# Eleven of 71 expert tiles spread over two step pairs, 16-bit routing marks, and the last values inside the branch arms

## What is computed

```python
x = L0_attn_x                        # (4, 1024, 128) f32
xn = _layernorm(x, axis=-1)
x = x + _L0_attn_ref(xn, W_q, W_k, W_v, W_o) + _L0_ffn_ref(xn, Wg, gamma, beta, W1, b1, W2, b2)
```

## Time and profile before

| | |
|---|---|
| median of 3 runs | 589.49 us (587.09 to 590.52) |
| the profiled execution | 589.15 us, its span 587.2 us |
| PE busy | 92% |
| ACT busy | 85% |
| DVE busy | 51% |
| POOL busy | 42% |
| TensorE clock, mean granted | 0.992 |

### The profile page before, as it was taken

How to read it: one execution, slowest core, us unless ns; L and a number is a source line. 1 busy time by engine, 2 the same in 40 slices (tenths; PEclk the granted TensorE clock), 3 DMA queues, 4 the chain that set the end, 5 groups by cost and what they waited for, 6 DMA issues and landing times.

```text
span 587.2 us, 12446 instructions
## 1 busy us (share of the span) xinstructions
PE 541.0 (92%) x4620; PEld 246.0 (42%) x4620; DVE 300.9 (51%) x1002; ACT 501.4 (85%) x552; POOL 246.0 (42%) x303
## 2 busy tenths in 40 slices
PE   8899988878999999999899999999989999999783
PEld 6323312222455554445345555434534555554111
DVE  4975789965434344463344433555433444343672
ACT  2699999989898788898888888899899888888992
POOL 4299900078646444556223444365521444322000
PEclk9999999999999999999999999999999999999996
DMA  7144320051435545324443464433433455460821
GB/s 257 29 138 123 113 62 11 1 181 49 159 108 165 185 149 162 99 75 149 136 133 105 163 211 153 141 100 100 160 98 114 154 176 188 142 188 30 315 81 39
DMA packets 44657, 75.47 MB, mean 129 GB/s; under 512 B 7585, under 2 KB 17873, under 8 KB 44081
## 3 DMA queue, kind: packets, MB, share of 16 engines
q1 hardware_dynamic: 39232, 63.71, 33.9%
q0 software_dynamic: 4544, 9.32, 5.2%
q10 hardware_dynamic: 816, 1.61, 0.7%
HBM read 33.88 MB, written 8.85 MB: 73 GB/s over the span
## 4 chain that ended last, share of the span: by engine, by line
PE 63%; ACT 21%; DVE 8%; issue 3%; DMA 2%; POOL 1%; SPq 1%; ACTq 1%; another core or an unknown queue 0%; POOLq 0%; DVEq 0%
PE acc L696 29%; ACT ring L921 20%; PE sc L661 11%; PE aside_bank L740 9%; PE sc L754 8%; PE aside_bank L768 2%; DMA sin<-rope_sin 2%; DVE xn L1228 2%; PE aside_bank L572 1%; PE sc L729 1%; DVE xn L1230 1%; DVE xn L1233 1%; PE aside_bank L588 1%; DVE blocks L1089 1%; SPq L332 1%
## 5 line engine op out<-in xcount | busy, mean ns | idle before, releaser
L921 ACT ACTIVATE ring<-sc 128x1024 f32<-128x1024 f32 x512 | 488.0, 1040 | 59.9 <-PE sc L661 55.9
L696 PE MATMUL acc<-ring,v 128*9 128x512 f32 x2048 | 250.9, 595 | 18.3 <-ACT ring L921 11.8
L513 POOL DMA_INDIRECT work<-normed,token x71 | 71.3, 1004 | 235.1 <-DVE work L1290 181.5
L661 PE MATMUL sc<-qs,ks 32*128 32x512 f16 x1024 | 101.4, 384 | 16.2 <-ACT ring L921 14.1
L1296 DVE TENSOR_SCALAR work<-aside_bank,xn 128x128 f32<-128x128 f32 x216 | 60.8, 345 | 107.1 <-PE aside_bank L740 105.8
L661 PEld LDWEIGHTS sc<-qs,ks 32*128 32x128 f16 x1024 | 26.2, 91 | 177.5 <-ACT ring L921 150.6
L696 PEld LDWEIGHTS acc<-ring,v 128*9 128x9 f32 x2048 | 39.9, 89 | 117.0 <-issue 76.5
L523 POOL DMA_INDIRECT token_out<-work,token x71 | 69.8, 983 | 37.6 <-issue 19.2
L740 PE MATMUL aside_bank<-work,xn 128*128 128x128 f32 x432 | 62.6, 288 | 0.0
L740 PEld LDWEIGHTS aside_bank<-work,xn 128*128 128x128 f32 x432 | 52.3, 191 | 12.2 <-issue 12.2
L754 PE MATMUL sc<-xn,work 128*128 128x128 f32 x432 | 57.2, 275 | 0.0
(11 more groups left out here) (194 smaller groups left out, 416.4 us busy)
## 6 DMA issues: line engine op xcount, KB each, us to landing
xn<-w_rest SPq DMA_DIRECT2D x54, 323.0 KB
xn<-L_ffn_W SPq DMA_DIRECT2D x54, 256.0 KB
w_last<-w_rest SPq DMA_DIRECT2D x17, 323.0 KB
w_last<-L_ffn_W SPq DMA_DIRECT2D x17, 256.0 KB
qs<-hl SPq DMA_DIRECT2D x60, 64.0 KB
ks<-hl SPq DMA_DIRECT2D x60, 64.0 KB
x<-L_attn_x SPq DMA_DIRECT2D x4, 512.0 KB, 8.2
w_rest<-L_ffn_W SPq DMA_DIRECT2D x8, 256.0 KB, 4.0
```

The source lines that it names most:

```text
L513: pool.indirect_dma_start(out=xt[t % TILE_BUFFERS], out_offset=None, in_=xh_d[:, :], in_offset=bass.IndirectOffsetOnAxis(ap=token[:, 0, t: ...
L661: last = nc.tensor.matmul(dst, ks[r:r + 32, kb * P:(kb + 1) * P], qs[r:r + 32, at], start=True, stop=not slow)
L696: last = nc.tensor.matmul(acc[32 * j:32 * j + VW, :], v9[:, b, kb, 4 * g + j, :], ring[:, (2 * n + j // 2) % UNITS, j % 2, :], start=(kb = ...
L921: nc.scalar.activation(ring[:, (2 * n + u) % UNITS, :, :], sc[HOME[2 * n + u]][:, :].rearrange("p (h c) -> p h c", h=2), ACT.Exp, scale=SC ...
```

## The change

1. `weigh(STEPS - 1)` and `project_out(B - 1, 1)` of PE stand in a function `finish`, called at the end of the last fast arm and at the end of each slow arm. DVE's code behind the arms stays.
2. The marks of the routing: indices and slots are held in bfloat16 (copied by POOL behind the stored rows), the column index runs outermost and the group of 8 innermost. PE reads each of the 8 matrices of a group with a step of 8 elements.
3. `place` sums by two instructions of `tensor_tensor_scan` in place of the doubling loops.
4. The tables: marks from step 26 and inversions from 29 to 36 without a gap, tokens at 36, owners at 37, plain projections at 38, 40, 46, 50, gates at 43, tiles from 42 to 238.
5. `TILE_AT` becomes `ONE_AT` (first layer) and `TWO_AT` (turn and second layer). Eleven tiles have them in two pairs: ONE at 54, 58, 72, 104, 118, 122, 136, 168, 182, 186, 200 and TWO at 56, 60, 74, 108, 120, 124, 138, 172, 184, 188, 202. TWO at 56, 120, 184 shares its iteration with the norms, TWO at 60, 124, 188 with the bound. There are 72 steps with a TWO, as there were 72 with a tile.
6. The loads of the results start at step 240 (before 238), the merges stand at 244, 246, 249, 250 (before 242, 245, 248, 251).

```diff
-ROUTE_AT, RANKS_AT, SLOTS_AT, OWNER_AT, GATES_AT = 21, 24, 24, 29, 39
-INVERT_AT = {n: g for g, n in enumerate((35, 37, 38, 40, 43, 44, 46, 47))}
-MARK_AT = {n: g for g, n in enumerate((32, 33, 35, 37, 40, 41, 43, 44))}
-TOKENS_AT = 47
-PLAIN_AT = {n: (1, r) for r, n in enumerate((28, 49, 50, 54))}
+ROUTE_AT, RANKS_AT, SLOTS_AT, OWNER_AT, GATES_AT = 21, 24, 24, 37, 43
+INVERT_AT = {n: g for g, n in enumerate(range(29, 29 + GROUPS))}
+MARK_AT = {n: g for g, n in enumerate((26, 27, 29, 30, 31, 32, 33, 34))}
+TOKENS_AT = 36
+PLAIN_AT = {n: (1, r) for r, n in enumerate((38, 40, 46, 50))}
-FFN_FROM = 52
-TILE_AT = {n: k for k, n in enumerate([n for n in range(FFN_FROM, STEPS, 2) if n not in TAKEN][:SLOT_TILES + 1])}
+FFN_FROM, FFN_TO = 42, 240
+SMALL = [n for at in (NORM_AT, FLAG_AT) for n in at]
+FREE = [n for n in PAIRS if n not in PLAIN_AT and n not in PROJECT_AT]
+HALVED = [(FREE[FREE.index(n) - 1], n) for n in SMALL]
+SPLIT_PAIRS = [n for pair in HALVED for n in pair]
...
+for n in FREE:
+    if n not in SPLIT_PAIRS or SPLIT_PAIRS.index(n) % 2 == 0:
+        ONE_AT[n] = len(ONE_AT)
+    if n not in SPLIT_PAIRS or SPLIT_PAIRS.index(n) % 2:
+        TWO_AT[n] = len(TWO_AT)
...
-SQUARE_AT.update({n: (1, r) for r, n in enumerate((53, 55, 56, 57))})
+SQUARE_AT.update({n: (1, r) for r, n in enumerate((43, 45, 50, 54))})
...
+            pool.wait_ge(xh_out, 16 * B)
+            nc.gpsimd.tensor_copy(all_places, iota_p.unsqueeze(2).to_broadcast([P, P, GROUP])).then_inc(indices_ok, 1)
+            nc.gpsimd.tensor_copy(all_tiles, iota_t[:, 0:SLOT_TILES].unsqueeze(2).to_broadcast([P, SLOT_TILES, GROUP])
+                                  ).then_inc(indices_ok, 1)
+            nc.gpsimd.tensor_copy(pick_16[:, :], pick_name).then_inc(indices_ok, 1)
...
-                    last = nc.tensor.matmul(bank[0][:, 0:2 * SLOT_TILES], place_mark[g % 2][:, i, :],
-                                            named[g % 2][:, i, :, :].rearrange("p v c -> p (v c)"),
+                    last = nc.tensor.matmul(bank[0][:, 0:2 * SLOT_TILES], place_mark[g % 2][:, :, i],
+                                            named[g % 2][:, :, :, i].rearrange("p v c -> p (v c)"),
...
-                if n in TILE_AT:
-                    tile(TILE_AT[n], n)
+                if n in ONE_AT:
+                    layer_one(ONE_AT[n])
+                if n in TWO_AT:
+                    layer_two_and_turn(TWO_AT[n], n)
...
                     following = attend(b, False)
                     if b + 1 < B:
                         batches(b + 1, following)
+                    else:
+                        finish()
                 with pe.Else():
                     for later in range(b, B):
                         attend(later, True)
+                    finish()
+
+            def finish():
+                weigh(STEPS - 1)
+                project_out(B - 1, 1)
 
             batches(0, flag_of(0))
-            weigh(STEPS - 1)
-            project_out(B - 1, 1)
...
-                a, far = 1, 1
-                while far < T:
-                    nxt = 3 - a
-                    nc.vector.tensor_copy(cnt[:, nxt, 0:far, :], cnt[:, a, 0:far, :])
-                    link(nc.vector.tensor_tensor(cnt[:, nxt, far:T, :], cnt[:, a, far:T, :],
-                                                 cnt[:, a, 0:T - far, :], ALU.add))
-                    a, far = nxt, 2 * far
+                link(nc.vector.tensor_tensor_scan(upto, not_first, totals, 0.0, ALU.mult, ALU.add))
...
+                link(nc.vector.tensor_tensor(tile_mark[k], all_tiles, slot_hl[:, 0, js].unsqueeze(1).to_broadcast(of_tiles),
+                                             ALU.is_equal))
+                nc.vector.tensor_tensor(place_mark[k], all_places,
+                                        slot_hl[:, 1, js].unsqueeze(1).to_broadcast([P, P, GROUP]), ALU.is_equal)
+                nc.vector.tensor_scalar(named[k][:, 0, :, :], tile_mark[k], row_name, None, ALU.mult)
+                nc.vector.tensor_tensor(named[k][:, 1, :, :], tile_mark[k],
+                                        pick_16[:, js].unsqueeze(1).to_broadcast(of_tiles), ALU.mult).then_inc(mark_ok, 1)
```

More of the change, by code:

```diff
@@ L98 @@
-SINE_AT = {n + 1 if n != 28 else 48: piece for n, piece in PLAIN_AT.items()}
+FFN_FROM, FFN_TO = 42, 240
+PAIRS = range(FFN_FROM, FFN_TO, 2)
+SMALL = [n for at in (NORM_AT, FLAG_AT) for n in at]
+FREE = [n for n in PAIRS if n not in PLAIN_AT and n not in PROJECT_AT]
+HALVED = [(FREE[FREE.index(n) - 1], n) for n in SMALL]
+SPLIT_PAIRS = [n for pair in HALVED for n in pair]
+MORE = len(FREE) - len(SMALL) - (SLOT_TILES + 1)
+assert len(set(SPLIT_PAIRS)) == 2 * len(SMALL) and MORE >= 0
+for m in range(MORE):
+    at = FREE.index(PER_BATCH + 8 + (STEPS - PER_BATCH) // (MORE + 1) * m)
+    while FREE[at] in SPLIT_PAIRS or FREE[at + 1] in SPLIT_PAIRS:
+        at += 1
+    SPLIT_PAIRS += [FREE[at], FREE[at + 1]]
@@ L99 @@
+ONE_AT, TWO_AT = {}, {}
+for n in FREE:
[3 more added lines that the diff above has]
+        TWO_AT[n] = len(TWO_AT)
+del ONE_AT[max(ONE_AT)]
+TWO_STEP = {k: n for n, k in TWO_AT.items()}
+assert len(ONE_AT) == SLOT_TILES and len(TWO_AT) == SLOT_TILES + 1
+SINE_AT = {n + 1: piece for n, piece in PLAIN_AT.items()}
 SQUARE_AT = {n + 5: piece for n, piece in PLAIN_AT.items() if piece[0] > 1}
-SQUARE_AT.update({n: (1, r) for r, n in enumerate((53, 55, 56, 57))})
@@ L101 @@
-SPLIT_ROUND = {piece: 3 if n < FFN_FROM + 4 else 5 + min(k for k, step in TILE_STEP.items() if step > n)
+SQUARE_AT.update({n: (1, r) for r, n in enumerate((43, 45, 50, 54))})
+SPLIT_ROUND = {piece: 3 if n < FFN_FROM else 5 + max(k for k, step in TWO_STEP.items() if step < n)
                for n, piece in SINE_AT.items()}
-WEIGHTS_AT = {n: k + 3 for n, k in TILE_AT.items() if k >= 1 and k + 3 < SLOT_TILES}
-LOAD_AT = TILE_STEP[SLOT_TILES] + 2
-MERGE_AT = {LOAD_AT + 4 + 3 * b: b for b in range(B)}
+WEIGHTS_AT = {n: k + 3 for n, k in TWO_AT.items() if k >= 1 and k + 3 < SLOT_TILES}
@@ L108 @@
+LOAD_AT = FFN_TO
+MERGE_AT = {LOAD_AT + n: b for b, n in enumerate((4, 6, 9, 10))}
 FRONT_BANK = (0, 1, 1, 1)
@@ L130, in bank_uses @@
             ("turn", TURN_AT), ("values", VALUES_AT), ("invert", INVERT_AT), ("plain", PLAIN_AT), ("norm", NORM_AT),
-            ("bound", FLAG_AT), ("out", PROJECT_AT), ("one", TILE_AT)) if n in at and at.get(n) != SLOT_TILES]
+            ("bound", FLAG_AT), ("out", PROJECT_AT), ("one", ONE_AT)) if n in at]
         pieces += [(name,) for name, at in (("wo", WO_AT), ("rows", COLUMNS_AT), ("ranks", RANKS_AT),
@@ L151, in score_homes @@
             order = [2] + order
-        before = n - 2 if n - 2 in TILE_AT else None
+        before = n - 2 if n - 2 in TWO_AT else None
         for u in range(2):
@@ L213, in build @@
         pick = work[:, 4 * T * E:6 * T * E].rearrange("p (a t e) -> p a t e", a=2, e=E)
-        rank = work[:, 6 * T * E:8 * T * E].rearrange("p (a t e) -> p a t e", a=2, e=E)
+        behind = work[:, 6 * T * E:7 * T * E].rearrange("p (t e) -> p t e", e=E)
+        totals, not_first = (work[:, k * T * E:(k + 1) * T * E] for k in (7, 8))
         turned = [sb(f"turned{k}", [P, CH]) for k in range(4)]
@@ L671, in maxima @@
                 wait(pe, e_ok, 2 * PER_QUAD * q)
-                wait(pe, tile_taken, len([n for n in TILE_AT if n < PER_QUAD * q]))
+                wait(pe, tile_taken, len([n for n in TWO_AT if n < PER_QUAD * q]))
                 pe.wait_ge(m_wide[b], 2 * (base + 1))
@@ L713, in ranks @@
                 enter_bank(0, "ranks")
-                nc.tensor.matmul(bank[0][:, 0:T * E], before, cnt[:, 0, :, :], start=True, stop=True)
+                nc.tensor.matmul(bank[0][:, 0:T * E], not_before, cnt[:, 0, :, :], start=True, stop=True)
                 nc.tensor.matmul(bank[0][:, T * E:2 * T * E], ones[:, :], cnt[:, 0, :, :], start=True, stop=True
```

93 lines of the change are left out of this document (39 added, 54 removed).

## The result

The changed kernel takes 597.44 us (median of 4 runs, 595.61 to 598.60) beside 588.29 us for the kernel before in the same round: a ratio of 1.0150, 95% interval [1.0103, 1.0196]. It is slower, where 584.4 us was forecast, and it lies outside the range, above its end of 589.6 us. The profiled execution took 595.61 us, its span 593.8 us; that is 6.6 us more than the span of 587.2 us before.

A forecast was written before the change was run, and what follows sets the result against it. It took a tile pair as bound by a loop through PE and ACT, 4.58 us. 589.15 - 3.7 (end) - 3.7 (tiles moved) + 2.4 (step 64) = 584.15 us, 584.4 us as median; range 579.0 to 589.6 us.

The forecast's parts named there:

- the price of the inversions: Routing: eight inversions in a row at 0.68 us each, making a step 1.92 us instead of 1.82 us, 0.8 us.
- rival (c): PE reads marks slowly, columns 16 bytes apart: inversions take twice 0.68 us, 4.9 us in all, 589.3 us; chance 0.14.
- Eleven tiles over two pairs: Tile pairs: a TWO pair alone still costs 4.58 us, a ONE pair stays at 3.65 us; gain nothing.
- Rival (a): PE sets the tile pairs: up to 0.9 us gained for each of eleven, 575 to 580 us; chance 0.10.
- Tiles from step 42: Four fewer tile pairs from step 64 on, 0.93 us each: 3.7 us less there, the same four dearer ahead.
- Step 64, 2.4 us later: Routing, steps 24 to 64: 80.4 us in place of 78.0 us; bounds -1 us and +9 us.
- (b): Marks on DVE stay at 2.87 us, routing ends late, PE 9.4 us late at step 37: 593.8 us; chance 0.09.
- new waits: PE's waits in the routing: 1.6, 0.8, 1.4 and 0.8 us, together 4.6 us, of which PE's lead absorbs 1.6 us.
- The mark at 1.7 us: Routing on DVE: a mark falls from 2.87 us to 1.7 us with 16-bit operands; bounds 1.2 and 2.87 us.
- POOL's copies 2.2 us: Ahead of mark 0: POOL's three copies take 2.2 us, between 1 and 4 us, and are done at 79.0 us.
- The end, 3.7 us less: Behind the last exponential: `weigh(255)` starts 2.1 us earlier, it and the projection run at full clock; at least 2.1 us.
- Rival (d): At the end: DVE's branch becomes the last wait, or the clock falls again; 2.1 us or less gained, 586 us; chance 0.17.

The follow-up runs named there:

- the last two runs: The kernel before with only the end moved into the arms, ratio 0.9951, and the changed kernel with a step of 2 and its end behind the arms, ratio 1.0070.
- the kernel with its end behind the arms: The changed kernel with marks at a step of 2 elements and the last values and projection behind all arms, as before: 589.10 us, ratio 1.0070.
- the kernel with only the weights at 8: The changed kernel with the step of 8 elements only in the inversions' weights, the moving operand contiguous from 32-bit instructions: 595.77 us, one execution.

## Why the prediction was wrong, point by point

**The step that failed is the price of the inversions.** The sum took the eight inversions at 0.68 us each and nothing for the way in which PE reads the marks. The prediction named that mechanism as rival (c), columns that lie 16 bytes apart, but with a chance of 0.14 and a price of 4.9 us, "if an inversion takes twice its 0.68 us". Measured, an inversion takes 3.3 times as long (2.25 us), 1.57 us more in each of eight steps, 10.9 us on the path. "Twice" rested on no row: no matmul of the trace reads with a step. An unknown without a row needs a bound that is far enough; the range ended at the price that I had chosen, "all of (c)", and so left out what happened. Put right in the prediction's sum for the profiled execution, 584.15 + 10.9 = 595.05 us, against a profiled 595.61 us.

**The rest of the sum held in its terms, but gave less than forecast.** With a step of 2, which takes this one term away, the kernel takes 585.03 us, where 584.4 us was forecast; that they lie so close is in part luck, since the kernel before was faster on that chip. The forecast was a ratio of 0.991, and measured is 0.9962 [0.9930, 0.9994]: of the 5.1 us forecast 1.6 us are missing by the medians and 2.9 us by the ratio. In the trace of that kernel the span is 2.9 us under that of before: 3.6 us for the later step 64, 4.0 us less to step 240, 0.4 us more to the last exponential's end, for which the sum had nothing, and 2.9 us less behind it. Term by term:

- *Eleven tiles over two pairs: nothing.* Right in the sum. ACT's timeline of the kernel after, steps 72 to 76:

```profile
182.91 1.94 ACT L955 ACTIVATE ring<-sc 128x1024 f32<-128x1024 f32 x2 [0.48 <-PE sc L693]
185.07 5.61 ACT L955 ACTIVATE ring<-sc 128x1024 f32<-128x1024 f32 x6 [0.22 <-PE sc L693]
191.16 1.02 ACT L955 ACTIVATE ring<-sc 128x1024 f32<-128x1024 f32 x1 [0.49 <-PE sc L693]
```

  The two pairs take 8.25 us (182.91 to 191.16), a whole tile pair and a plain one 4.59 + 3.65 = 8.24 us. Not as I had it in detail: the ONE pair takes 3.98 us, not ACT's 3.65 us, and the TWO pair 4.27 us, not 4.58 us, just under the 4.3 us set as its sign. It is the order of the pairs that sets this and not the split: with the tile whole in the second pair both last as long, and in the kernel before pair 66, which has no tile and follows one, takes 3.98 us and pair 70, which has one and follows a plain pair, 4.27 us. Rival (a) is out.
- *Tiles from step 42: 3.7 us less behind step 64.* 4.4 us less in the changed kernel, 4.2 us between the last two runs, which share a chip. Right, and as forecast it is paid back ahead of step 64.
- *Step 64, 2.4 us later.* 14.1 us later, and outside its own bound of 9 us, which was made for (b) alone. Repaired it is 3.6 us later, 1.2 us more than forecast. Its new waits were priced at 4.6 us together and come to 4.9 us. The wait at step 32 is as priced, 1.56 us. Steps 30 to 37 take 2.02 us on the average without it, 0.2 us over the plain 1.82 us, where 0.1 us was priced. At the first tile PE waits 1.71 us for DVE, where 2.2 us was priced for step 40 and the first tile; this wait comes behind a DVE instruction that takes 1.6 us more than usual (last section). The other 0.9 us, in what PE's lead absorbs and in the squares, was not traced.
- *The mark at 1.7 us.* Right: marks 0 and 1 start at 79.78 and 81.53 us. `place` also ended as worked out (79.7 us, 79.4 us forecast), and the larger scan takes 0.69 us.
- *POOL's copies 2.2 us, done at 79.0 us.* Right: 1.04, 0.94 and 0.23 us, the last from 78.82 us.
- *The end, 3.7 us less.* Right. The kernel after, from the last exponential's end at 585.97 us:

```profile
586.02 1.04 PE L728 MATMUL acc<-ring,v 128*9 128x512 f32 x8 [0.79 <-ACT ring L955]
587.13 0.72 DVE L1123 STREAM_TRANSPOSE blocks<-acc 128x512 f32<-128x512 f32 x1 [3.35 <-PE acc L728]
...
589.27 1.36 PE L795 MATMUL aside_bank<-woT,oT 128*128 128x128 f32 x8 [2.20 <-DVE oT L1133]
590.66 0.69 DVE L1304 TENSOR_TENSOR x<-aside_bank,x 128x512 f32<-128x512 f32 x1 [1.45 <-PE aside_bank L795]
```

  4.69 us from there to the last addition, 8.15 us before: 3.5 us less. `weigh(255)` starts 0.05 us behind the exponential. The projection kept the full clock only in some runs: it takes 1.36 us here at a granted clock of 0.80, 1.16 us at 0.97 in the first kernel with only the end moved, 1.88 us at 0.56 in the second, and 1.92 us at 0.55 with a step of 2. Rival (d) is out for DVE's branch; its falling clock is there in some runs and worth up to 0.8 us.

**What the change is worth without the flaw.** The kernel before with only the end moved is 0.9945 and 0.9951 of the kernel before, as fast as anything tried here. The 16-bit marks, the scans, the new tables and the split tiles bring nothing that these runs can measure. My reading, which no run tests by itself, is that a tile costs its pair 0.93 us wherever it stands, and that the routing was not on the path except through the tiles that it lets start.

**What stays open.** Why the kernel before takes 588 to 589.5 us on two chips and 584.8 us on two others. In the traces from the first two, between 1 and 7 us of steps 64 to 239 are pairs that last longer than their like elsewhere, mostly by about half a microsecond and at most by 1.6 us; in those from the others there are none. I didn't follow what releases them. In the sums across chips this is an error of a few us. Nor was it tried whether the second stop of PE goes away when the code is shifted.

## What to carry to other kernels

A layout that gives one engine its fast rate sets the step at which the next engine reads: price the reader as well as the writer, and choose the innermost group as small as the writer's fast rate allows (two 16-bit elements were enough here for both). When no row of the trace shows a form of access, don't let the range end at the price you picked for it. And work that only moves along a path that is full from end to end brings nothing; here the one gain was an idle time that ended in a branch.

## What the hardware showed that I had not expected

- A bfloat16 moving operand of 142 columns costs PE, for eight matmuls, 0.68 us contiguous, 0.71 us with 4 bytes between columns, 1.23 us with 8 and 2.18 to 2.25 us with 16; a step of 16 bytes in the weights costs 47 ns a load, nearly all of it hidden.
- PE can stop twice behind one late branch: 3.07 us and, four matmuls later, 2.42 us, in the trace of the kernel with its end behind the arms.
- A DVE instruction whose median is 0.29 us took 1.88 us at 115.71 us of the kernel after, beside one of POOL's gathers (115.16 us). PE's next wait for DVE is shown below it:

```profile
115.71 1.88 DVE L1130 TENSOR_TENSOR att<-blocks,rec 128x128 f32<-128x128 f32 x1
...
119.08 0.33 PE L761 MATMUL aside_bank<-const,work 128*128 128x128 f32 x1 [1.72 <-DVE rotated L1292]
```

  It is not a matter of one execution: in each of the eight traces with the tight table one such instruction takes 1.82 to 1.93 us, and in none of the six others does one take more than 0.83 us. So it belongs to what the tight table costs; why it is slow was not followed.
- In the kernel with only the weights at 8, PE waited twice for DVE among the marks (1.96 us until 84.68 us, 2.14 us until 95.24 us), and its granted clock, 0.997 over the changed kernel, was 0.57 to 1.00 in windows of 4 us there. Two of the windows, the clock third from the right:

```profile
84.00:88.00 4.00, 3.32 (x26) 1.48 (x27) 3.93 (x8) 1.52 (x3) 0.00 (x0) 0.72 0.00 0
...
96.00:100.00 4.00, 4.00 (x29) 1.25 (x25) 3.93 (x9) 1.94 (x2) 0.00 (x0) 0.57 0.00 0
```

  The eight matmuls of an inversion take 1.17 us behind these waits and 0.74 us elsewhere, so a late mark costs twice: the wait, and the matmuls behind it, part of them at the 1.2 GHz level.
